# Four attention and relation layers on 16 graphs: weights loaded before the masks, row counts taken from the weight sums, one mean product, layer 0's output finished a slot later

## The reference

```
x = norm(x + L0(x)); x = norm(x + L1(x)); x = norm(x + L2(x)); x = norm(x + L3(x))

L0: h = x W0^T;  e_ij = leaky(h_i.a_left + h_j.a_right), masked where adj is 0
    softmax over j;  out_i = sum_j alpha_ij h_j          (a row with no edge: mean of h)
L1: the same with W1 and a1, softmax over i (columns), then elu
L2: h = x W2^T + b2, biases on the scores, softmax over j, then elu
L3: y = (adj == 1) x w3[0] + ... (adj == 4) x w3[3] + b3
```

## Time and profile before

| | |
|---|---|
| time, median of 3 runs | 482.32 us (481.08 to 482.47) |
| the profiled execution | 483.51 us, span 481.7 us |
| PE busy | 390.6 us (81%), PEld 343.3 (71%) |
| DVE busy | 380.5 us (79%) |
| ACT busy | 359.3 us (75%) |
| POOL busy | 286.5 us (59%) |
| TensorE's granted clock, mean | 0.957 of 2.4 GHz |

### The profile page before, as it was taken

One profiled execution on the slowest core, in us unless ns is written; L12 is line 12 of the kernel. 1 busy time (PEld: TensorE's weight loads), 2 busy tenths in 40 slices (PEclk: granted clock), 3 DMA queues, 4 the chain that ended last, 5 costly groups with the idle time before them and its releaser, 6 DMA issues. The chain is left out here.

```text
span 481.7 us, 10006 instructions
## 1 busy us (share of the span) xinstructions
PE 390.6 (81%) x3154; PEld 343.3 (71%) x3161; DVE 380.5 (79%) x1384; ACT 359.3 (75%) x869; POOL 286.5 (59%) x425
## 2 busy tenths in 40 slices
PE   0279999999997987767667788999999959989870
PEld 0279998989996876656657677998999957545440
DVE  0123787878899889999999976788888997888862
ACT  1187687989867879889889886767777775787764
POOL 4033567877774345344353455777777885887883
PEclk9995999999998879999999999999999998999995
DMA  8995045320000000000000000000000000011112
GB/s 201 216 316 119 7 84 84 54 42 2 1 3 1 1 1 1 2 1 1 0 2 1 1 3 0 2 2 1 2 2 0 2 3 0 1 66 67 66 68 89
DMA packets 8759, 18.24 MB, mean 38 GB/s; under 512 B 1280, under 2 KB 2560, under 8 KB 8704
## 3 DMA queue, kind: packets, MB, share of 16 engines
q0 software_dynamic: 2304, 8.39, 9.5%
q1 hardware_dynamic: 2976, 4.52, 2.8%
q10 hardware_dynamic: 3424, 4.66, 2.7%
HBM read 21.76 MB, written 4.19 MB: 54 GB/s over the span
## 5 line engine op out<-in xcount | busy, mean ns | idle before, releaser
L458 PE MATMUL o_ps<-h_scaled,PT 128*128 128x129 f32 (+1 forms) x1536 | 190.2, 284 | 18.5 <-POOL h_scaled L239 15.6
L458 PEld LDWEIGHTS o_ps<-h_scaled,PT 128*128 128x128 f32 x1536 | 182.9, 199 | 21.1 <-issue 18.0
L671 ACT ACTIVATE X<-y,offset,rstd 128x128 f32<-128x128 f32 x256 | 104.8, 480 | 11.8 <-POOL offset L258 11.7
L891 DVE SCALAR_TENSOR_TENSOR PT<-rows_ps,factors,MT 128x512 f32<-128x512 f32 x128 | 89.3, 739 | 0.0
L246 POOL TENSOR_TENSOR var_eps<-mean_var,eps_tile 128x4 f32<-128x4 f32 x64 | 12.9, 201 | 119.7 <-DVE mean_var L965 119.7
L249 POOL TENSOR_TENSOR rstd<-var_eps,neg_half 128x4 f32<-128x4 f32 x64 | 65.2, 1019 | 5.0
L394 PE MATMUL h_ps<-wx,xT 128*128 128x130 f32 x384 | 63.7, 305 | 2.9 <-DVE smax L859 0.5
L394 PEld LDWEIGHTS h_ps<-wx,xT 128*128 128x128 f32 x384 | 54.3, 204 | 12.8 <-issue 11.4
L958 DVE BATCH_NORM_STATS2 stats<-y 128x6 f32<-128x128 f32 x256 | 55.7, 280 | 4.9
L644 ACT ACTIVATE edge<-edge,col_tmp,col_full 128x512 f32<-128x512 f32 x64 | 48.4, 802 | 12.6 <-DVE edge L871 12.5
L239 POOL TENSOR_TENSOR h_scaled<-hx,factors 128x516 f32<-128x516 f32 x32 | 33.6, 1051 | 36.8 <-ACT factors L621 26.4
(11 more groups left out here) (101 smaller groups left out, 682.9 us busy)
## 6 DMA issues: line engine op xcount, KB each, us to landing
MT<-adj_by_j POOLq DMA_DIRECT2D x16, 512.0 KB, 7.3
X<-x SPq DMA_DIRECT2D x16, 256.0 KB, 16.2
out<-X ACTq DMA_DIRECT2D x16, 256.0 KB, 2.0
w_rel<-w SPq DMA_DIRECT2D x1, 256.0 KB, 20.1
wx<-w_by_input ACTq DMA_DIRECT2D x1, 192.0 KB, 3.8
w_back<-w_by_output ACTq DMA_DIRECT2D x1, 192.0 KB, 4.8
bias<-b ACTq DMA_DIRECT2D x1, 64.0 KB, 12.9
bias<-b SPq DMA_DIRECT2D x1, 64.0 KB, 22.9
```

The lines of the kernel that those rows point to most:

```text
L458: last = pe.matmul(o_ps[it.b][:, ic, first:1 + D], PT[:, it.b, jc, ic * P:(ic + 1) * P], h_scaled[:, it.b, jc, first:1 + D], start=(jc == ...
L671: last = act.activation(X[:, g, c, :], y[:, b, c, :], ACT.Identity, bias=offset[:, b, c:c + 1], scale=rstd[:, b, c:c + 1])
L891: dve.scalar_tensor_tensor(out=PT[:, it.b, c, :], in0=rows_ps[:], scalar=factors[:, it.b, 1, c:c + 1], in1=m, op0=ALU.max, op1=ALU.mult, * ...
```

## The change

1. **Start.** ScalarE's queue issues w_back, a_cols and wx first; w_in counts these three. The three bias transfers count on b_in. GpSimd waits for w_in before the first mask. SP issues x0 and x1 at once, and from there on x of graph n only when the mask of graph n-2 has landed; w_rel and bias3 come last. The bias product (line 371) moves to TensorE's slot -1, its copy to ScalarE's slot -1, and split_bias2 to the head of VectorE's slot 0. VectorE's early wait for wa goes.
2. **Empty rows.** The 16 products of line 424 go. `row_sums` compares the weight sum in o_ps with 0 instead. So empty_row is known a slot or more later, and `mean` and `add_residual` of layer 0 move on GpSimd from item n+1 to item n-1. The wait for the mask goes from `project` to `weights`.
3. **Mean.** One product of 128 columns for two of 64; h_ps is laid out as two banks with two chunks of 130 columns each, and the mean or the spread maximum behind them. `h_mean` has eight buffers for two, and `take_h` waits for the `mean` of eight items before.
4. **Layer 0 a slot later.** `take_out`, `finish`, `aggregate`, rstd and offset of layer 0 handle item n-2 for n-1, `take_norm` item n-3 for n-2. take_out of item n-2 and attend of item n use the same o_ps, so attend waits for y_sum of n-2. On GpSimd rstd and offset of layer 1 too handle item n-2 for n-1, at a place ahead of layer 1's scale_h.
5. **Flags.** `flag` handles item n for item n+4.

```diff
         def _(sp):
             for n in range(G):
+                if n >= 2:
+                    sp.wait_ge(sem(f"mask_in{n - 2}"), 16)
                 load_x(item(n))
-                if n == 3:
-                    sp.dma_start(w_rel[:, :, :], ...)
-                    sp.dma_start(bias3[:, :], ...)
+            sp.dma_start(w_rel[:, :, :], ...)
+            sp.dma_start(bias3[:, :], ...)
...
-        W_IN = 16 * 6
+        W_IN, B_IN = 16 * 3, 16 * 3
...
# GpSimd, attention_slot
-                if at(1) and at(1).l != 1:
+                if at(-1) and at(-1).l == 0:
+                    mean(at(-1))
+                    add_residual(at(-1))
+                if at(1) and at(1).l == 2:
                     mean(at(1))
                 if at(-1) and at(-1).l == 2:
                     elu_low(at(-1))
-                if at(-2) and at(-2).l == 2:
+                if at(-2):
                     find_rstd(at(-2))
                     find_offset(at(-2))
-                if at(-1) and at(-1).l != 2:
-                    find_rstd(at(-1))
-                if at(-1) and at(-1).l != 2:
-                    find_offset(at(-1))
-                if at(1) and at(1).l == 0:
-                    add_residual(at(1))
                 if at(1) and at(1).l == 1:
                     scale_h(at(1))
...
+            pool.wait_ge(sem("w_in"), W_IN)
             for g in range(8 + FIRST):
                 load_mask(item(g))
...
# TensorE
-                    for e in range(2):
-                        last = pe.matmul(h_mean_ps[:, e, :], x_sum[...], wx[:, l, e * 64:(e + 1) * 64], ...)
+                    last = pe.matmul(h_mean_ps, x_sum[...], wx[:, l, 0:D], ...)
...
-                if it.l == 0:
-                    pe.wait_ge(sem(f"mask_in{it.g}"), 16)
...
-                if it.l == 0:
-                    for ic in range(C):
-                        for jc in range(C):
-                            last = pe.matmul(h_ps[:, ic, 130:131], MT[:, it.g, jc, ic * P:(ic + 1) * P],
-                                             ones_bf[:, 0:1], start=(jc == 0), stop=(jc == C - 1))
...
# attend
                 pe.wait_ge(sem("h_scaled"), it.done)
+                if it.done > 2 and item(it.done - 3).l == 0:
+                    pe.wait_ge(sem("y_sum"), it.done - 2)
...
+                if n == -1:
+                    pe.wait_ge(sem("b_in"), B_IN)
+                    pe.matmul(o_ps[1][:, 0, 0:2], bias2_col..., a_cols[:, 2, :], ...).then_inc(sem("b2_ps"), 1)
...
# ScalarE
-            act.dma_start(wx[:, :, 0:D], w_in).then_inc(sem("w_in"), 16)
             act.dma_start(w_back[:, :, :], w_out).then_inc(sem("w_in"), 16)
             act.dma_start(a_cols[:, :, :], a_in).then_inc(sem("w_in"), 16)
+            act.dma_start(wx[:, :, 0:D], w_in).then_inc(sem("w_in"), 16)
...
-                    if it.l > 0 or it.g >= 2:
-                        act.wait_ge(sem("mean_raw"), halves(it) - 2)
+                    if it.l > 0 or it.g >= 8:
+                        act.wait_ge(sem("mean_raw"), halves(it) - 8)
...
-                if at(-2) and at(-2).l < 2:
+                if at(-3) and at(-3).l != 1:
+                    take_norm(at(-3))
+                if at(-2) and at(-2).l == 1:
                     take_norm(at(-2))
-                if at(-3) and at(-3).l == 2:
-                    take_norm(at(-3))
...
-                if at(4) and at(4).l == 0:
-                    flag(at(4))
+                if at(0) and at(0).l == 0:
+                    flag(at(0))
...
# VectorE
-                if n == FIRST:
+                if n == 0:
                     split_bias2()
...
-                if at(-1) and at(-1).l != 1:
+                if at(-2) and at(-2).l == 0:
+                    take_out(at(-2))
+                if at(-1) and at(-1).l == 2:
                     take_out(at(-1))
                 if at(-2) and at(-2).l == 2:
                     add_elu(at(-2))
+                if at(-2) and at(-2).l != 1:
                     finish(at(-2))
                 if at(1):
                     weights(at(1), (0, 1))
-                if at(-2) and at(-2).l == 2:
+                if at(-2) and at(-2).l != 1:
                     aggregate(at(-2))
                 if at(-1) and at(-1).l == 1:
                     add_elu(at(-1))
-                if at(-1) and at(-1).l != 2:
+                if at(-1) and at(-1).l == 1:
                     finish(at(-1))
                 if at(1):
                     weights(at(1), (2, 3))
```

More of the change, by code:

```diff
@@ L23 @@
 LAYERS = 3
-S1, S2, DEG = 129, 130, 131
+S1, S2 = 129, 130
 FIRST, ALL_STEPS = -4, 2 + G * (LAYERS + 1)
@@ L71, in build @@
         hx = sb("hx", [P, 4, C, 132])
-        h_mean = sb("h_mean", [P, 2, D])
+        h_mean = sb("h_mean", [P, 8, D])
         h_scaled = sb("h_scaled", [P, 2, C, 132])
@@ L128, in build, with h_chunk_ps, halves_of @@
         xT_ps = pb("xT_ps", [P, N])
-        h_ps = pb("h_ps", [P, C, 256])
+        h_ps = pb("h_ps", [P, 2, 512])
         rows_ps = pb("rows_ps", [P, N])
         o_ps = [pb(f"o_ps{b}", [P, C, 256]) for b in range(2)]
-        h_mean_ps = h_ps[:, 2:4, 132:196]
-        smax_ps = h_ps[:, 0:2, 132:196]
+        h_all_ps = h_ps[:, :, 0:260].rearrange("p k (c w) -> p k c w", c=2)
+        smax_ps, h_mean_ps = h_ps[:, 0, 260:260 + P], h_ps[:, 1, 260:260 + D]
+        def h_chunk_ps(c, width):
+            return h_ps[:, c // 2, (c % 2) * 130:(c % 2) * 130 + width]
         sums_ps = (xT_ps, rows_ps)
         block = ctx.enter_context(nc.Block())
+        def halves_of(chunks):
+            return chunks.rearrange("p (k c) w -> p k c w", k=2)
         def pipeline(slot, begin, end, items):
@@ L369, in _ @@
             for l in range(LAYERS):
-                pe.matmul(xT_ps[:, 2 * l:2 * l + 2], w_back[:, l, :], a_cols[:, l, :], start=True, stop=True)
-            pe.matmul(xT_ps[:, 6:8], bias2_col[:, 0:1].broadcast_to([P, P]), a_cols[:, 2, :],
-                      start=True, stop=True).then_inc(sem("wa_ps"), 1)
+                last = pe.matmul(xT_ps[:, 2 * l:2 * l + 2], w_back[:, l, :], a_cols[:, l, :], start=True, stop=True)
+            last.then_inc(sem("wa_ps"), 1)
             pe.wait_ge(sem("ident"), 1)
@@ L710, in attention_slot @@
                     take_xT(at(4))
-                if at(4) and at(4).l == 0:
-                    flag(at(4))
+                if n == -1:
+                    act.wait_ge(sem("b2_ps"), 1)
+                    act.copy(b2_a[:, :], o_ps[1][:, 0, 0:2]).then_inc(sem("b2_a"), 1)
+                if at(0) and at(0).l == 0:
+                    flag(at(0))
             def relation_slot(at, n):
@@ L747, in redo @@
                         if l != 1:
-                            act.activation(h_mean[:, 0, :].rearrange("p (e d) -> p e d", e=2), h_mean_ps, ACT.Copy,
+                            act.activation(h_mean[:, 0, :], h_mean_ps, ACT.Copy,
                                            scale=1.0 / N).then_inc(sem("re_h_mean"), 1)
-                        act.copy(hx[:, 0, :, 1:131], h_ps[:, :, 0:130]).then_inc(sem("re_hx"), 1)
+                        act.copy(halves_of(hx[:, 0, :, 1:131]), h_all_ps).then_inc(sem("re_hx"), 1)
                         act.wait_ge(sem("re_smax"), k)
@@ L858, in take_max @@
                 dve.wait_ge(sem("smax_ps"), it.done)
-                dve.tensor_reduce(smax[:, it.b:it.b + 1], smax_ps, AX.XY, ALU.max).then_inc(sem("smax"), 1)
+                dve.tensor_reduce(smax[:, it.b:it.b + 1], smax_ps, AX.X, ALU.max).then_inc(sem("smax"), 1)
             def column_terms(it):
@@ L912, in row_sums @@
                 dve.wait_ge(sem("att"), it.done)
+                if it.l == 0:
+                    dve.tensor_scalar(empty_row[:, it.g, :], o_ps[it.b][:, :, 0], 0.0, None, ALU.is_equal)\
+                        .then_inc(sem("empty_row"), 1)
                 dve.tensor_scalar(z_row[:, it.b, :], o_ps[it.b][:, :, 0], TINY, None, ALU.max)\
@@ L1083, in redo @@
                         dve.wait_ge(sem("re_max_ps"), k)
-                        dve.tensor_reduce(smax[:, 0:1], smax_ps, AX.XY, ALU.max).then_inc(sem("re_smax"), 1)
+                        dve.tensor_reduce(smax[:, 0:1], smax_ps, AX.X, ALU.max).then_inc(sem("re_smax"), 1)
                         if l == 1:
```

53 lines of the change are left out of this document (27 added, 26 removed).

## The result

The changed kernel takes 474.5 us (472.7 to 474.5) where the kernel before, on the same chip, takes 481.7 (480.1 to 482.5). The ratio is 0.9861, 95% interval 0.9817 to 0.9905. Timed again beside the experiments it took 472.7 us, ratio 0.9841 [0.9801, 0.9882]. The forecast was 469.8, its own range 464 to 476. The profiled execution took 474.5 us with a span of 472.7, 9.0 less than before in both. One further execution of the changed kernel took 733.5 us at a granted clock of 1.00; it is left out as a slow one, and why it was slow isn't known.

The account below looks back on a forecast made before the run. It took late weights to set the start, TensorE to bound layer 0, VectorE layer 1, a VectorE-TensorE loop layer 2. Terms -15 - 3.5 + 4 + 0.5 + 1.5 = -12.5 gave 471.0 profiled, 469.8 us median, range 464 to 476.

Parts of the forecast that it names:

- The start: Fill before attend(1): weights' transfers ahead of the masks bring attend(0) and attend(1) earlier, -15 us, bounds -10 and -19.
- split_bias2 at 1.5: Start, VectorE's slot 0: split_bias2 ahead of take_max, for which project(3) waits, costs 1.5 us.
- x2's wait: Start: x2, issued only when mask 0 has landed, keeps TensorE waiting 1.5 us, bounds 0 and 5.
- rival (a): Start still set by transfers, each x behind a mask; start gives 7 for 15, total 478 us; chance 0.08.
- The flags: Start: flags of items 0 to 3 leave ScalarE; of their 8 us, 3 on the path, bounds 1 and 6.
- Layer 0's slot: Slot falls from 6.70 to 6.45 us, bound by layer 2's VectorE-TensorE loop; 14 slots give -3.5 us, bounds -7.5 and 0.
- the mask's issue covered: Layer 0, GpSimd: a mask's issue of 0.6 us in half the slots is covered by its waiting for mean_var.
- From layer 0 to layer 1: Slots 15 to 17: column_terms ahead of take_out, and item 15's output in slot 17; +4 us, bounds +2 and +8.
- Only the first of them is late: Seam of layers 0 and 1: only the first of slots 15 to 17 has attend late behind take_out, by 2.8 us.
- Layer 1: VectorE sets the slot; TensorE's two gaps merge into one of 2.5 us; +0.5 us, bounds 0 and +8.
- rival (c): Merged gap drops TensorE to 1.2 GHz in all of layer 1: +30, total 499 us; chance 0.05.
- From layer 1 to layer 2: Earlier elu_low gains 1.7 us; take_norm waits 2 to 3 us in slots 31 to 33; +1.5, bounds -1.5 and +4.

Follow-up runs that it names:

- the late-split run: The changed kernel with three edits (layer 1's rstd/offset, take_out order, earlier x2 and x3), plus split_bias2 moved to the end of slot 0: 460.2 us, 0.9549.
- the run with the start alone: The kernel before with only the new transfer order, late bias and late flags; counts, two mean products and old layer order kept: 474.6 us, 0.9864.
- the order turned: The changed kernel with layer 0's take_out ahead of layer 1's column terms on VectorE instead of behind them: 471.2 us, 0.9783.
- the run with filler products: The changed kernel with eight unread 124-column identity products per slot of layer 1, filling TensorE's gap before the own maxima: 474.9 us, 0.9893.
- the kernel with the three edits: The changed kernel with layer 1's rstd/offset for item n-1, take_out ahead of column terms, x2 and x3 behind the weights alone: 461.3 us, 0.9598; again 462.2.

## Why the prediction came out as it did

- **The start** (-15 forecast, -14.5 and -16.0 measured at attend(1)). The sum was right and several of its parts were not. Transposes at 7.0: measured 7.31. split_bias2 at 1.5: 1.09 of waiting, and the late-split run gives back 1.05. x2's wait was taken at 1.5 with 5 as the bound: 4.94, the bound itself, and undoing it gave 4.8 to 5.3 at attend(0). So far rival (a) was right, but only for x2: x3 and x4 were there in time. The flags were put at 3 us of gain. No run has them alone, but in the trace of the kernel before the waits of TensorE in the fill that stand behind a flag are two, 0.82 us for the factors (at 32.25) and 0.57 for the own maximum (at 33.47), so 3 was too much. attend(0) came at 30.59 and 30.03 for the 28.6 forecast, and attend(1) was still in time since slot 0 took 6.9 and 6.0 us instead of 8.8, while the sum had let it stay. What made up for all this had no term: I had put the whole of the products' worth into layer 0's slot, 0.40 us for the counts, but in the start they stand between each projection and hx, and the run with the start alone puts what it leaves out at 5.4 us or more. That the total of the start came out is luck.
- **Layer 0's slot** (6.45 forecast, 6.22 measured; -3.5 forecast for 14 slots, -7.4 measured for 13). As forecast, TensorE binds no longer, and the loop of layer 2 fits what is left. The term was mis-sized by 0.23 a slot. Part of it is the time from smax to the output, 85.56 - 85.27 = 0.29 us here; I carried over the loop of layer 2, where the reciprocal has to wait its turn and it is 350.16 - 349.70 = 0.46. The rest is in the old slots, which were not all 6.70. I had read one slot, where TensorE is the bound. Slots 4 to 7 of the kernel before took 7.21 to 7.37 us (72.14 to 101.14, 29.0 for four). In them GpSimd still issues a mask, ahead of mean_term, and ScalarE, which needs a free h_mean buffer, waits a microsecond for mean_term. One of these slots:

```profile
87.37 0.64 POOL L202 DMA_DIRECT2D MT<-adj_by_j  x1
...
90.17 0.28 ACT L598 ACTIVATE h_mean<-h_ps 128x128 f32<-128x128 f32 x1 [1.01 <-POOL mean_term L215]
```

After the last mask's issue (94.58) the wait is 0.33 us and the slot 6.7. So the prediction was wrong to call the mask's issue covered; by these rows I estimate its cost at 29.0 - 4 x 6.71 = 2.2 us. The run with the start alone, which keeps two h_mean buffers, still takes 7.2 in slots 5 to 7. In the changed kernel, with eight buffers, no slot is over 6.22. No run changes the buffers alone.

- **From layer 0 to layer 1** (+4 forecast, bounds to +8; +5.1 and +6.4 measured). "Only the first of them is late" was wrong: attend waits 3.38, 3.38 and 2.86 us in slots 15, 16 and 17, and each time it takes 5.3 to 5.5 us for 3.8, so that the forecast 8.9 us from attend to attend become 11.0 and 10.4. With the order turned the waits go to another place and some 2 us come back. That the remaining 4 us are the price of a third slot that carries layer-0 output beside layer-1 work fits VectorE's busy time, 36.0 us for 32.0 in the stretch, but no run shows it.
- **Layer 1** (+0.5 forecast; +1.4 and +0.6 measured). The prediction had called itself wrong if the clock fell often in layer 1. It did, in every second slot, behind the merged gap, and cost nothing in the steady part, as the run with filler products shows; rival (c) is refuted by it. Not foreseen: the slot got 0.14 us shorter, by the other collision of VectorE with GpSimd. The loss is in the slots at both ends of the layer.
- **From layer 1 to layer 2** (+1.5 forecast, bounds to +4; +6.2 and +5.4 measured). This is the step that failed, beyond its own bound. The waits of take_norm were foreseen in kind and size (2.82 to 3.66 us against "2 to 3"), but I let slot 34 catch up and set 1.7 us of gain against them. Putting rstd and offset back brought the stretch to 37.88 us: the waits had been on the path, and the earlier elu sum gave 0.4 us at most, the difference to the 38.27 of before.
- **Layer 2 and the relation layer** (0 and 0): -0.3 and within 0.4.

The sum was missed by 3.5 us in the profiled execution (471.0 forecast, 474.5) and by 4.7 in the median, less in the second timing. By the terms of the first profile the seams were missed by 1.1 and 4.7 us, layer 1 by 0.9 and the start by 0.5, against 3.9 that layer 0 gave beyond its term. That errors of 7 and of 4 us partly cancelled is luck, too.

## What to carry to other kernels

When a step is moved a slot later to make a loop tight, price it at the loop's ends too: here layer 0 gained 7.4 us, by all that the change did in it, and the two seams lost 11. Ask of each part of a move what it gives: putting layer 1's rstd and offset back, the part of the move that its loop didn't need, gave back 5.8 to 6.6 us at the seam for 0.15 us a slot in the layer. A sum that comes out right proves no term in it: in the start, a wait three times as long as forecast was hidden by a gain that stood nowhere. Read more than one slot of a loop before pricing it: four of layer 0's old slots had another bound than the one I read. The busiest engine of a loop need not be its bound; give it more work and take some away before believing it.

## What the hardware showed that was not expected

- TensorE's granted clock fell to half after a single gap of 2.65 us in a busy loop (0.50 from 217 to 219 us), and did not after gaps of 1.2 to 1.4, nor after one of 1.91 us that ended at 269.4. At the seam it fell at 278.3, behind waits of 0.58 and 1.56 us with four products between them. In layer 1 it came back within the slot.
- The same program's start differs by up to 3.1 us from run to run (attend(1) at 29.57 and 32.67 in the kernel with the three edits) though TensorE's first product (5.37, 5.40) and first transpose (7.23, 7.27) are at the same times and no transfer is waited for behind them. The third set of four transposes starts at 13.88 and 13.91 and takes 0.66 us in one and 1.12 in the other, with a granted clock of 1.00 in the windows of both; later the clock is 0.50 from 24 to 27 us in the slower one alone. So in the start the granted clock doesn't tell all of how fast the products run.
- A VectorE instruction of 4 columns took 0.78 to 1.04 us instead of 0.21 beside a scaling on GpSimd, in each steady slot of layer 1. Small instructions are not safe from such a collision.
